# An attention-and-feed-forward kernel whose batch-1 preparation, attention bias and late modulations change place

## The reference, cut to what is computed

```python
mod = (silu(c) @ wmod).reshape(2, 6, 1, 256)          # six modulations for each of 2 batches
sa, ca, ga, sb, cb, gb = (mod[:, j] for j in range(6))
ga, gb = sign(ga) * max(|ga|, 0.25), sign(gb) * max(|gb|, 0.25)
h = layernorm(x) * (1 + ca) + sa                      # x: (2, 1024, 256)
# 16 heads of 128: q, k, v = h @ W + b; rotary; causal softmax; out @ Wo + bo
x = x + ga * attention(h)
h = layernorm(x) * (1 + cb) + sb
x = x + gb * (silu(h @ Wgate.T) * (h @ Wup.T)) @ Wdown.T   # 704 hidden, integer weights
```

## Time and profile before

| | |
|---|---|
| median of 3 runs | 1103.43 us (1103.32 to 1105.03) |
| the profiled execution, first to last instruction | 1100.9 us |
| TensorE busy | 1053.1 us (96%) |
| VectorE, ScalarE, GpSimd busy | 807.6, 672.6, 615.8 us |
| mean granted TensorE clock | 0.992 of full |
| first piece of unit 0 on TensorE | 44.44 us |
| first piece of unit 1 on TensorE | 74.13 us |

### The profile page before, as it was taken

One profiled execution on the slowest core, in us unless ns is written; L12 is line 12 of the kernel. 1 busy time (PEld: TensorE's weight loads), 2 busy tenths in 40 slices (PEclk: granted clock), 3 DMA queues, 4 the chain that ended last, 5 costly groups with the idle time before them and its releaser, 6 DMA issues.

```text
span 1100.9 us, 20576 instructions
## 1 busy us (share of the span) xinstructions
PE 1053.1 (96%) x6624; PEld 917.1 (83%) x6624; DVE 807.6 (73%) x1451; ACT 672.6 (61%) x1443; POOL 615.8 (56%) x474
## 2 busy tenths in 40 slices
PE   6889999999999999999999999999999999988798
PEld 5778888888888888888888888888888888877676
DVE  6767877677767777787777776777677777769765
ACT  5466666566656666666566666666666666655642
POOL 3155655565556656565656555565566555674643
PEclk9899999999999999999999999999999999999999
DMA  9212211221112211211122111211122111320001
GB/s 282 68 36 61 49 30 40 68 48 38 31 31 68 48 39 40 67 44 34 31 68 48 39 39 31 68 39 39 40 67 49 39 37 31 107 78 1 11 29 39
DMA packets 41707, 56.60 MB, mean 51 GB/s; under 512 B 5204, under 2 KB 24724, under 8 KB 41620
## 3 DMA queue, kind: packets, MB, share of 16 engines
q1 hardware_dynamic: 41620, 55.30, 19.5%
HBM read 19.63 MB, written 2.10 MB: 20 GB/s over the span
## 4 chain that ended last, share of the span: by engine, by line
PE 76%; DVE 8%; POOL 6%; issue 5%; DMA 3%; ACT 2%; SPq 1%; DVEq 0%; ACTq 0%; POOLq 0%
PE ps_r L1179 14%; PE ps_r L1181 14%; PE ps_r L1180 14%; PE ps_t L1304 9%; PE ps_s L1179 5%; PE ps_s L1181 5%; PE ps_s L1180 5%; DMA swapped<-straight 2%; POOL swapped L566 2%; POOL straight L567 2%; PE ps_s L1186 2%; PE ps_s L1189 2%; POOL w_lo L559 1%; DVE v_lo L963 1%; PE ps_s L1289 1%
## 5 line engine op out<-in xcount | busy, mean ns | idle before, releaser
L566 POOL TENSOR_TENSOR swapped<-swapped,sin_sb 128x512 f32<-128x512 f32 x124 | 164.2, 1325 | 269.9 <-DMA swapped<-straight 269.7
L765 ACT ACTIVATE pT_hi<-ps_t 128x512 fp32r<-128x512 f32 (+3 forms) x384 | 187.8, 490 | 114.5 <-PE ps_t L1304 110.0
L1031 DVE TENSOR_TENSOR pT_lo<-ps_t,pT_hi 128x512 fp32r<-128x512 f32 (+3 forms) x384 | 204.1, 549 | 60.4 <-ACT pT_hi L765 55.0
L1055 DVE TENSOR_REDUCE neg_max<-ps_s 128x1 f32<-128x128 f32 (+7 forms) x256 | 192.1, 751 | 59.8 <-PE ps_s L1289 59.3
L573 POOL TENSOR_TENSOR qk_lo<-straight,qk_hi 128x512 fp32r<-128x512 f32 x124 | 158.8, 1290 | 130.5 <-ACT qk_hi L689 130.5
L776 ACT ACTIVATE probs<-ps_s,neg_max 128x128 f32<-128x128 f32 (+7 forms) x256 | 190.0, 742 | 23.8 <-DVE neg_max L1055 22.8
L1304 PE MATMUL ps_t<-ident,probs 128*128 128x128 f32 x1152 | 185.3, 274 | 7.5 <-DVE pT_lo L1031 7.4
L567 POOL TENSOR_TENSOR straight<-straight,cos_sb 128x512 f32<-128x512 f32 x124 | 178.8, 1442 | 0.0
L957 DVE TENSOR_TENSOR straight<-straight,swapped 128x512 f32<-128x512 f32 x126 | 133.8, 1062 | 27.9 <-POOL straight L567 27.6
L1179 PE MATMUL ps_s<-qk_hi 128*128 128x512 f32 (+3 forms) x384 | 141.9, 370 | 0.4 <-ACT probs L776 0.4
L1047 DVE SCALAR_TENSOR_TENSOR y<-ps_r,inv_sum,y 128x256 f32<-128x256 f32 x256 | 111.8, 478 | 34.0 <-PE ps_r L1181 29.5
(11 more groups left out here) (181 smaller groups left out, 2334.7 us busy)
## 6 DMA issues: line engine op xcount, KB each, us to landing
swapped<-straight SPq DMA_DIRECT2D x252, 128.0 KB, 2.3
x_in<-in_L_attn_x SPq DMA_DIRECT2D x4, 512.0 KB, 5.3
w_raw<-in_L_attn_Wk SPq DMA_DIRECT2D x8, 256.0 KB, 3.7
w_raw<-in_L_attn_Wq SPq DMA_DIRECT2D x8, 256.0 KB, 3.9
w_raw<-in_L_attn_Wv SPq DMA_DIRECT2D x8, 256.0 KB, 3.3
wo_all<-in_L_attn_Wo SPq DMA_DIRECT2D x1, 2048.0 KB, 11.5
wo_raw<-in_L_attn_Wo SPq DMA_DIRECT2D x8, 256.0 KB, 2.7
x<-in_L_attn_x SPq DMA_DIRECT2D x4, 512.0 KB, 4.1
```

Of the source, the lines that this page charges most:

```text
L566: pool.tensor_tensor(swapped[:, q, :], swapped[:, q, :], sin_sb[:, cs], ALU.mult)
L765: nc.scalar.activation(turned_at(ORDER[step], k0, k1)(pT_hi), ps_t[:, (T_FIRST[step] + j) % 2, 0:(k1 - k0) * P].rearrange("p (k q) -> p k ...
L1031: nc.vector.tensor_tensor(turned_at(t, k0, k1)(pT_lo), ps_t[:, (T_FIRST[step] + j) % 2, 0:(k1 - k0) * P].rearrange("p (k q) -> p k q", q=P ...
L1055: nc.vector.tensor_reduce(neg_max[:, t:t + 1], ps_s[:, step % 2, 0:(t + 1) * P], AX, ALU.max, negate=True).then_inc(max_ready, 1)
```

## The change

Ahead of unit 0 only batch 0 is prepared. Unit 0 gets plans of its own:

```diff
+OPENING_TENSOR = """make:K0+ make:Q0+ scores:0 make:X4 make:X5 scores:1 make:X6 make:X7 scores:2 make:P0- turn:0.0 make:P1-
+        scores:3 turn:1.0 make:K1+ scores:4 turn:1.1 turn:2.0 make:Q1+ scores:5 turn:3.0 turn:3.1 make:B make:V0
+        turn:4.0 scores:6 make:V1 turn:5.0 scores:7 turn:5.1"""
+OPENING_SCALAR = """out:K0+ out:Q0+ exp:0 out:X4 out:X5 exp:1 out:X6 out:X7 high:P0- turn:0.0 exp:2 high:P1- high:K0+
+        high:Q0+ turn:1.0 out:K1+ turn:1.1 exp:3 turn:2.0 exp:4 out:Q1+ turn:3.0 exp:5 turn:3.1 turn:4.0 high:V0
+        high:K1+ high:V1 turn:5.0 exp:6 split:O turn:5.1 high:Q1+"""
+OPENING_VECTOR = """max:0 max:1 low:P0- add:K0+ max:2 turn:0.0 add:Q0+ low:P1- max:3 turn:1.0 sum:B max:4 turn:1.1 turn:2.0
+        max:5 turn:3.0 add:K1+ turn:3.1 fill:B turn:4.0 max:6 low:V0 add:Q1+ low:V1 max:7 turn:5.0 turn:5.1"""
+OPENING_POOL = """norm:2 norm:3 low:X4 low:X5 rotate:K0+ rotate:Q0+ low:X6 low:X7 low:K0+ low:Q0+ rotate:K1+ rotate:Q1+ low:K1+
+        low:Q1+ split:O"""
```

```diff
+            def normalise(n):
+
+                pool.wait_ge(rstd_ready, 1)
+                for t in range(4 * n, 4 * n + 4):
+                    ins = pool.tensor_scalar(xn[1][:, t - NQ, :], x_in[:, t, :], mv[:, t, 0:1], rstd[:, t:t + 1],
+                                             ALU.subtract, ALU.mult)
+                ins.then_inc(xn_ready, 1)
...
-            roots(1, slice(0, NTT // 2))
+            for n in range(2):
+                roots(n + 1, slice(4 * n, 4 * n + 4))
             mod_out(0)
...
-            norm(x_in, lambda t: xn[:, t, :], range(NTT // 2), lambda n: dve.wait_ge(x_ready[n], 16), xn_ready)
...
+            for n in range(2):
+                norm(x_in, lambda t: xn[0][:, t, :], range(4 * n, 4 * n + 4), x_arrived, xn_ready)
...
+            def bias_half():
+
+                dve.wait_ge(wo_all_ready, 16)
+                link(nc.vector.tensor_scalar(bias_sum[:, :], wo_all[:, HEADS // 2, :],
+                                             cols[:, COL_BV + HEADS // 2:COL_BV + HEADS // 2 + 1], None, ALU.mult))
+                for h in range(HEADS // 2 + 1, HEADS):
+                    ins = nc.vector.scalar_tensor_tensor(bias_sum[:, :], wo_all[:, h, :], cols[:, COL_BV + h:COL_BV + h + 1],
+                                                         bias_sum[:, :], ALU.mult, ALU.add)
...
             for n in range(GROUPS4 // 2):
                 turn_xn(n)
+                if n == GROUPS4 // 2 - 2:
+                    pe.wait_ge(s_rows_ready, 80)
+                    turn_rows(s_rows, SROWS, 2)
+                    pe.wait_ge(wmod_b_ready, 64)
+                    modulation(1, (2, 3))
+            modulation(1, (4, 5))
             pe.wait_ge(w_ready[WK], 1)
             for n, piece in enumerate(FIRST_QK):
...
-            turn_xn(GROUPS4 // 2)
-            turn_xn(GROUPS4 // 2 + 1)
-
-            pe.wait_ge(cols_ready, 2)
-            pe.wait_ge(wo_all_ready, 32)
-            for h in range(HEADS):
```

More of the change, by code:

```diff
@@ L113, in unit_plan @@
                 out.append((what, which, n))
+        elif name == "B":
+            out.append((what, v, ("bias",)))
+        elif name[0] == "X":
+            out.append((what, v, ("x", int(name[1]))))
+        elif what == "norm":
+            out.append((what, v, (int(name),)))
         elif name[0] in "KQ":
@@ L153, in __init__, with work @@
         self.units = range(first, last) if i is None else range(first + UNITS, last + UNITS)
-    def work(self, plan):
-        return [x for u in self.units for x in unit_plan(plan, u)]
+    def work(self, plan, unit=None):
+        return [x for u in self.units if unit in (None, u) for x in unit_plan(plan if u else OPENING[plan], u)]
     def count(self, n, per_round):
@@ L261, in build @@
         newton = small("newton", [P, NTT], F32)
+        ones = small("ones", [P, 1], F32)
         neg_max = small("neg_max", [P, NQ], F32)
@@ L482, in run @@
                     n = u // UNITS + 1
-                    qk = [piece for what, _, piece in unit_plan(TENSOR_PLAN, u) if what == "make" and piece[0] == "qk"]
+                    qk = [piece for what, _, piece in ps.work(TENSOR_PLAN, u) if what == "make" and piece[0] == "qk"]
                     for piece in qk:
@@ L589, in run @@
                         rotate(ps, piece)
+                    elif what == "norm":
+                        normalise(*piece)
+                    elif what == "low" and piece[0] == "x":
+                        h_low_b(piece[1])
                     elif what == "low":
@@ L796, in do @@
                 elif what == "out":
[L797 removed]
+                    {"qk": qk_out, "gate": gate_out, "x": h_out_b}[piece[0]](ps, piece)
                 else:
@@ L1062, in do @@
                     turn_low(ps, x, *piece)
+                elif what == "sum" and piece[0] == "bias":
+                    bias_half()
+                elif what == "fill":
+                    bias_fill(ps, piece)
                 else:
@@ L1247, in make @@
                                     k == 0, k == n_keys - 1)
+                elif piece[0] == "x":
+                    k, chunk = piece[1] % KT, piece[1] // KT
+                    pe.wait_ge(xn_ready, chunk + 1)
+                    for t in range(4):
+                        ins = nc.tensor.transpose(dst[:, t * P:t * P + P],
+                                                  xn[1][:, 4 * chunk + t - NQ, k * P:k * P + P], ident[:, :])
+                elif piece[0] == "bias":
+                    pe.wait_ge(wo_all_ready, 16)
+                    for h in range(HEADS // 2):
+                        nc.tensor.matmul(dst[:, 0:DIM], cols[:, COL_BV + h:COL_BV + h + 1].broadcast_to([P, P]),
+                                         wo_all[:, h, :], start=h == 0, stop=False)
+                    pe.wait_ge(bias_sum_ready, 1)
+                    ins = nc.tensor.matmul(dst[:, 0:DIM], ones[:, :].broadcast_to([P, P]), bias_sum[:, :],
+                                           start=False, stop=True)
                 elif piece[0] == "gate":
@@ L1312, in turn_rows, with modulation @@
                     .then_inc(cols_turned, 1)
-            def modulation(n):
-                for j in ((0, 1), (2, 3, 4, 5))[n]:
+            def modulation(n, parts):
+                for j in parts:
                     for k in range(KT):
```

166 lines of the change are left out of this document (91 added, 75 removed).

## The result

The changed kernel takes 1119.56 us, median of four runs (1118.26 to 1120.19). The kernel before takes 1103.61 in the same rounds, the ratio is 1.0138 with an interval of 1.0119 to 1.0156. So the change costs 15 to 16 us. The forecast was 1109.7: slower was right, and the time lies 5 us above the upper end of the range.

What follows compares the result with a forecast made beforehand. TensorE, busy for 96% of the span, was taken as the bound. F 26.5 + 22.5 + 24.9 + 1.5 + 2.0 + 3.0 put unit 1 at 80.4 against 74.13: 1103.4 + 6.3 = 1109.7 us, range 1100.5 to 1114.5.

Steps and rivals of the forecast that it cites:

- F: Mark 1, start of the first piece in the preamble: 16.6 + 3.2 + 6.7 = 26.5 us (21.5 to 26.7).
- GpSimd's eight normalising steps: Unit 0, ahead of GpSimd's other work: 690 ns each, at most +5.5 us on VectorE's nine steps, 3.0 taken.
- the fourth maximum: Mark 3, its end in unit 0: s1+13.5 where it was s1+12.0, so +1.5 us (0 to +3).
- sum:B: Eight VectorE steps ahead of the turn of step 3: 3.6 us, plus up to three GpSimd waits; +2.0 taken.
- from unit 1 on nothing is changed: Behind unit 0: TensorE has no room, so a shift of unit 1's first piece moves the end by as much.
- The slow modulations: 32 records ahead of the first piece, 0.22 us each at 1.2 GHz: 7.0, less 0.3 of waiting, +6.7 us.
- The 3.2 us for the layer norm: Preamble, norm in two chunks: +1.5 for repeated small steps, +1.9 beside GpSimd's low weights; +3.2 taken (+1.4 to +3.4).
- the transfers cost nothing: Preamble loads: 3 MB up to the late modulations, 15 us, wanted near 19; 2 MB of tables wanted at 33.
- s1: Start of step 1's wide score tile: F+22.5 = 49.0 us (F+17.5 to F+25), against 49.19 before.
- Rival (c): Worse: stalls followed by 1.2 GHz stages (+1.3 us), contest paid in full (+3.6): 1114.6, chance 0.18.
- its sister page: "GPSIMD Engine Reference": two-input or 2-port VectorE steps contend with GpSimd; sum:B and nine rotary steps held in full, 1113.
- mark 2: The way from F to s1 through VectorE's rotary chain, with 3.0 us for contest against GpSimd's normalising (0 to 5.5).

Runs made afterwards that it cites:

- e3: Changed kernel with the s-row turning and late modulations moved behind the two first value pieces on TensorE; 1113.77 us, ratio 1.0103.
- e5: Changed kernel with scores:1 ahead of make:X4 and make:X5 in TensorE's plan, nothing else; 1119.31 us, ratio 1.0132.
- e7: Changed kernel with sum:B moved between max:0 and max:1 in VectorE's plan; 1112.55 us, ratio 1.0083.
- e8: Changed kernel with 24 waits on a long-reached semaphore ahead of TensorE's last branch, shifting the code; 1117.26 us, ratio 1.011.
- c3: Changed kernel with c2, e3 and e2 together, and e6's sum behind max:1; 1110.3 us, ratio 1.0047.
- c5: c4 with sum:B between max:0 and max:1 on VectorE and exp:1 behind out:X7 on ScalarE; 1101.3 us, ratio 0.9984.
- e6: e4 with the sum's first step written as a product of two tiles; 1118.64 us, ratio 1.0122.
- e4: Changed kernel with sum:B right behind max:1 in VectorE's plan instead of ahead of max:4; 1119.08 us, ratio 1.0144.
- e2: Changed kernel with batch 0's layer norm in one go over eight tiles instead of two chunks; 1121.76 us, ratio 1.0154.
- e1: Changed kernel with batch 1's normalising back on VectorE, right behind its reciprocal roots; 1117.14 us, ratio 1.0121.
- c2: Changed kernel with batch 1's normalising on VectorE behind its first rotary chain, and scores:1 ahead of make:X4 and make:X5; 1115.74 us, ratio 1.0093.
- c4: c3 with the old x load order, ScalarE's batch 1 roots and VectorE's reciprocals later, and 24 waits before TensorE's last branch; 1101.18 us, ratio 0.9973.

## Why the prediction was right and where it was wrong

The direction was right, and so was F. Three steps failed. GpSimd's eight normalising steps were priced at 5.5 us and as a burden on VectorE only; they took 12.5 us, and the end of GpSimd's row, later for it, set the fourth maximum (3.1 us). sum:B and what follows it was too small (2.7 us). And "from unit 1 on nothing is changed" was taken for the time too (3.0 us).

**F: right, 27.03 for 26.5.** The slow modulations were priced at 0.22 us a record and took 6.99 us for 32; e3, without them ahead of F, has it 7.65 us earlier. The 3.2 us for the layer norm came out as 3.68 (first scaled tokens at 16.68), with GpSimd's low weights in the way as said (3.35 us for four steps). But the sentence "the transfers cost nothing" failed: I summed the bytes and didn't ask what stands behind what. The chunks that I charged are the cover of that move, and undoing them alone makes F and unit 1 later, not earlier.

**s1: right in size, by luck.** F+23.5 measured, F+22.5 forecast. What held it was a wait that my sum doesn't have. I had VectorE's nine rotary steps paying for GpSimd's one-input steps. They hardly did: most of them took 0.68 us and the chain ended at F+19.2, 2.8 us ahead of where I had it with the contest. s1 came 4.3 us behind the chain's end, since make:X4 stands ahead of it and waited 3.52 us for GpSimd; with scores:1 first (e5) s1 is F+20.0. For X4 and X5 I had +0.5, for ScalarE's banks. On GpSimd the contest was paid, up to 2.7 us a step while VectorE was in the row, and its steps without any contest took 1.21 us, where I had 0.69 from the earlier trace rows. That row is one operation on another type with constants as scalars, this one has a column for each of its two scalars; it was the nearest row, and it was off by 1.8. Eight steps made 12.5 us, 9.7 of their own and 2.8 of contest, not 5.5.

**The fourth maximum: wrong, s1+16.6 for s1+13.5, and the sum was built on the wrong chain.** I followed TensorE, ScalarE and VectorE from s1. e5 moves s1 by 4.3 us and the maximum by 0.1. What ended last was GpSimd's row, at 63.45: add:K0+ had its inputs, was shut out until the row ended, and took 2.82 us, for which I had 1.8. With the eight steps at 5.5 us GpSimd would have been 7 us earlier at the rotary products, and the row over by some 60.0 us: ScalarE's last tile for it was done at 58.73, and one low part takes 1.26 (an estimate from the timelines of after). add:K0+, which started at 61.18, would not have met it. I had written that "ScalarE's eight and GpSimd's twelve new operations cost what stands above; both have room", by busy sums over the stage. The room was behind the row, not ahead of what waits.

**sum:B: right in kind, too small.** 6.4 us for 5.6, and 8.14 from the fourth maximum to the turn for 7.05. In e7, without the sum there, that stretch is 4.30 us. Rival (c) had the rest: each stall followed by a stage at 1.2 GHz. It was priced at 1.3 us for one stage. In after the granted clock was 0.50 from 50.5 to 53.3 and from 58 to 61, and 0.66 from the turn of step 3 at 75.28 to 80. There the turn took 1.73 us and make:B's first sixteen products 4.46, where they took 0.93 and 3.62 in e7. From that turn to unit 1 it took 12.5 us, where the forecast had 10.9 and e7 has 11.9. The low clock after a stall varies from run to run: the same sixteen products took 5.79 us in e8, which is the same program up to there.

**The end: not foreseen at all, +3.0.** The forecast took "from unit 1 on nothing is changed" for the time as well as for the work. The second pause at the branch, 2.5 us, isn't in the diff, and 0.5 us more is scatter.

The deviations add up: F +0.5, s1 +1.0, fourth maximum +3.1, turn +1.1, unit 1 +1.6, the end +3.0, less 0.5 since the median lies 2.0 above the span and not 2.5: 9.8, and the forecast was off by 9.9. The range, whose upper end lies even a little below rival (c)'s 1114.6, was too narrow because that end added contests and clock to a chain that was taken as known; the chain itself was the uncertain thing.

The Trainium skill's page "SBUF — State Buffer" (section "SBUF: two separate sides") says that the shared ports are an exclusive lock: whichever of a VectorE operation with two SBUF inputs and a GpSimd operation starts first has them for its whole instruction, and the other is blocked. The turns in c3 to c5 agree in that the two alternate. One turn of both lasted some 1.42 us there, though, less than the 0.49 and 1.26 of the two alone together, so each wasn't held for the other's whole instruction. The 9.04 us of e6 don't agree: eight GpSimd instructions ended before the step was let in, not one. Nor does e7, where VectorE's two-input steps took 0.58 us in the middle of GpSimd's row. In the prediction I gave 1113 as the time by the rule of its sister page; by it the rotary steps of mark 2 would have been held in full, and they were not.

What stays open: why a VectorE step was shut out for the whole row of GpSimd's in e4 and e6 and took turns with it in c3 to c5. In the latter VectorE was at work when the row began, in the former it came 0.7 and 1.2 us behind its start. But add:K0+, which came while the row was going on, waited for its end in after, e2, e3, e5 and e8 (2.4 to 4.2 us), and was let in behind one operation in e1, c2 and e7 (1.4 to 1.6 us). The order of arrival therefore doesn't explain all of them.

## What to carry to other kernels

When work moves to another engine, put it into that engine's queue and read off what stands behind it and who waits for that; a sum of busy times says nothing about this. Undo parts one at a time, and then undo the loads and the small steps that came along: here the layer norm's chunks looked like a cost and were a cover, and late roots and the load order were together worth 6 us at unit 1 (c3 to c4), more than the normalising (2.6 in c2). Gains of single parts don't add when each uncovers another wait: c3 had five of them and lay over 10 us above their sum. An idea can be good although its first version is slower, but here the gain that was left is small: 8.8 us in the preamble became 2.5 at unit 1.

## What the runs showed of the hardware that I had not expected

- A VectorE step on SBUF can be shut out by a row of GpSimd's two-input operations for the whole row: 9.34 us for a one-input step, 9.04 for a two-input one, 0.34 to 0.49 when alone. add:K0+ (128x512, two inputs, 0.68 alone) took 2.4 to 4.2 us in five kernels and each time ended some 0.55 us behind the row. In other rows the two alternate: 1.38 us a step for VectorE, 1.45 for GpSimd (1.26 alone).
- Beside GpSimd's one-input steps VectorE lost next to nothing (median 0.58 us a step for 0.49, e7). GpSimd's single steps stretched from 1.21 to 2.7 us beside VectorE's rotary chain, and only to 1.23 to 1.36 beside the sum (e7). Eight of them lasted 12.4 to 12.6 us in every run, with the sum beside them or without.
- GpSimd takes 1.21 us to normalise 128x256 with two columns as scalars, VectorE 0.40.
- TensorE's first 512-wide products take 0.63 us, the same as at a granted clock of 0.50 (before, 45 to 48), where the granted clock of the table says 1.00 (after, 27.10 to 29.00). They reach 0.39 some 2.3 to 4.4 us behind F in before, e3, c4 and after. In after TensorE had been busy from 18.18 on without a gap, with modulations and turns, and it made no difference.
- TensorE can pause a second time, for 2.0 to 2.5 us, behind the first product of a branch, and 24 idle instructions ahead of the branch took the pause away (e8, c4, c5).
